# Four stages of an eight-stage transformer kernel re-arranged: ternary weights made beside the attention ahead, a local transformer's loads and residual beside its neighbours, its up-projection rests packed in one chunk, fourteen expert buffers

## The reference

```
x = x + L0_xattn(_layernorm(x), ctx)      # 16-head attention to 77 context rows
x = x + L0_ffn(_layernorm(x))             # ternary weights, 8-bit activations
x = x + L1_xattn(_layernorm(x), ctx)
x = x + L1_ffn(_layernorm(x))
x = x + L2_xattn(_layernorm(x), ctx)
x = x + L2_ffn(_layernorm(x))             # a whole local transformer, DEPTH = 6
x = x + L3_xattn(_layernorm(x), ctx)
x = x + L3_ffn(_layernorm(x))             # 64 experts, top 8, capacity 64
```

```
# L0_ffn: bitlinear(x, w) = act_quant(x) @ weight_quant(w).T
#   weight_quant: scale = 1 / clip(mean(|w|), 1e-5);  clip(round(w*scale), -1, 1) / scale
#   act_quant:    scale = 127 / clip(max(|x|, token), 1e-5); clip(round(x*scale), -128, 127) / scale
#   y = bitlinear(silu(bitlinear(x, w_gate)) * bitlinear(x, w_up), w_down)     inner width 1024
# L2_ffn: six times  x = x + local_attention(x);  then
#   hg = layernorm(x, g, bln) @ W1 + b1;  a, gate = split(hg)                  682 columns each
#   x = x + a * gelu(gate) @ W2 + b2
# L3_ffn: each token goes to 8 of 64 experts (256 -> 192 -> 256), their weighted results are summed
```

## Time and profile before

| | |
|---|---|
| median of three runs (lowest, highest) | 4475.44 us (4472.94, 4483.0) |
| the profiled execution: its time, its span | 4467.25 us, 4465.4 us |
| busy share of the span: PE, DVE, ACT, POOL | 89%, 56%, 44%, 33% |
| mean granted TensorE clock | 0.949 of full speed |
| share of the span of the DMA queue of SP | 13.2% |

### The profile page before, as it was taken

One profiled execution on the slowest core, in us unless ns is written; L12 is line 12 of the kernel. 1 busy time (PEld: TensorE's weight loads), 2 busy tenths in 40 slices (PEclk: granted clock), 3 DMA queues, 4 the chain that ended last, 5 costly groups with the idle time before them and its releaser, 6 DMA issues. The chain is left out here.

```text
span 4465.4 us, 70044 instructions
## 1 busy us (share of the span) xinstructions
PE 3960.8 (89%) x27065; PEld 2109.1 (47%) x27065; DVE 2515.2 (56%) x3505; ACT 1960.9 (44%) x3522; POOL 1468.7 (33%) x1326
## 2 busy tenths in 40 slices
PE   6767994869999999999999999999999999989564
PEld 4433431535554455445554455445554455435332
DVE  3583445548862588328862588328862588325522
ACT  3434544436643366326643366326643366314221
POOL 0000000016740376206640466206640467100044
PEclk9888997889999999999999999999999999999777
DMA  3000000021120111101120111101120111000377
GB/s 113 29 0 22 0 0 19 11 76 28 30 58 17 26 30 30 59 13 28 30 56 19 27 29 30 59 14 26 30 61 14 27 29 30 21 19 11 98 236 208
DMA packets 101435, 185.27 MB, mean 41 GB/s; under 512 B 13957, under 2 KB 54401, under 8 KB 100097
## 3 DMA queue, kind: packets, MB, share of 16 engines
q1 hardware_dynamic: 92912, 168.88, 13.2%
q0 software_dynamic: 6144, 9.44, 1.1%
q10 hardware_dynamic: 2064, 2.62, 0.2%
HBM read 112.06 MB, written 20.09 MB: 30 GB/s over the span
## 5 line engine op out<-in xcount | busy, mean ns | idle before, releaser
L1510 PE MATMUL PS<-locw,X 128*128 128x512 f32 x2304 | 1066.3, 599 | 43.9 <-PEq L1422 28.3
L1777 POOL TENSOR_TENSOR locm<-locm 128x512 f32<-128x512 f32 x384 | 488.1, 1271 | 920.2 <-DVE locm L1714 919.8
L1510 PEld LDWEIGHTS PS<-locw,X 128*128 128x128 f32 x2304 | 395.0, 190 | 456.6 <-issue 324.8
L1891 PE MATMUL PS<-locxn,locw 128*114 128x512 f32 (+1 forms) x1152 | 501.4, 593 | 13.4 <-DVE loch L2000 13.4
L1783 POOL TENSOR_TENSOR locm<-locm,locrn 128x512 f32<-128x512 f32 x384 | 392.4, 1043 | 129.0 <-ACT locrn L1629 129.0
L1790 POOL TENSOR_TENSOR locpr<-locpr,locrs 128x512 f32<-128x512 f32 x384 | 390.9, 1039 | 128.8 <-DVE locrs L1743 108.9
L1712 DVE TENSOR_TENSOR locm<-PS,loctab 128x512 f32<-128x512 f32 x384 | 263.6, 687 | 211.3 <-ACT locsq L1619 211.3
L1650 ACT ACTIVATE locpt<-PS 128x512 f32<-128x512 f32 x384 | 208.4, 594 | 321.8 <-PE PS L1520 321.8
L1891 PEld LDWEIGHTS PS<-locxn,locw 128*114 128x114 f32 (+1 forms) x1152 | 203.8, 178 | 306.8 <-issue 283.3
L2000 DVE SCALAR_TENSOR_TENSOR loch<-PS,locvec,locgl 114x512 f32<-114x512 f32 x144 | 107.0, 750 | 376.8 <-PE PS L1891 331.1
L1654 ACT ACTIVATE locpr<-locpr 128x1024 f32<-128x1024 f32 x192 | 203.3, 1059 | 191.4 <-DVE locpr L1734 191.4
(11 more groups left out here) (317 smaller groups left out, 6219.3 us busy)
## 6 DMA issues: line engine op xcount, KB each, us to landing
locve<-locva SPq DMA_DIRECT2D x372, 128.0 KB, 2.2
locw<-in_L2f_wqkv SPq DMA_DIRECT2D x36, 512.0 KB, 10.0
BIG<-in_L3f_gu SPq DMA_DIRECT2D x24, 768.0 KB, 5.6
BIG<-in_L3f_down SPq DMA_DIRECT2D x24, 384.0 KB, 6.9
moe_sums<-none SPq DMA_DIRECT2D x2, 4352.0 KB, 23.5
moeroom<-moe_sums SPq DMA_DIRECT2D x16, 512.0 KB, 6.9
locw<-in_L2f_w SPq DMA_DIRECT2D x6, 1364.0 KB
loctab<-in_L2f_tabs SPq DMA_DIRECT2D x6, 1024.0 KB, 10.3
```

The source lines that it names most:

```text
L1510: mm = pe.matmul(PS[:, o % 2, :], k.X[:, j, at - j:at - j + P], W[:, j, col:col + G], start=j == 0, stop=j == KD - 1)
L1777: pool.tensor_tensor(M1[:, j, :], M1[:, j, :], M2[:, x, :], ALU.add).then_inc(s.paired, 1)
L1891: mm = pe.matmul(PS[0:r, 4 + 2 * (m % 2) + half, :], W1[:, c, half * FI + m * FR:half * FI + m * FR + r], XNL[:, g % 2, c, :], start=c == ...
```

## The change

- **L0x and L0f.** The three weight loads are issued by SP behind L0x's own. DVE takes the three sums of absolute values in the steps of tiles 3, 4 and 5 of L0x, and the reciprocal in that of tile 7; POOL adds over the partitions and makes the ternary weights in BIG. L0f's first block is gone.
- **L0f's loop** is written out and deeper: gate and up in halves of 512 with their own semaphores, two buffers for most tiles, the x side done for two tiles at once, `down` three steps and `add` four steps behind. Scaling and rounding of x went from DVE to ACT (`raise_x`), of the hidden tile from DVE to POOL (`raise_h`), the small factors to POOL. PE turns XN directly.
- **L2f's start.** The layer norm is called by the stage, writes into X itself (`dest`), and SP's loads and POOL's mask cast and tables stand in its block; DVE waits there first for X to be saved.
- **L2f's up-projection.** Five chunks of 128 columns per half, and the two rests of 42 columns in one chunk: a in the rows 0 to 41, gate in the rows 64 to 105 of one bank, two matmuls for both.
- **L2f's end.** The saved residual is loaded in the last feed-forward block, once the attention outputs are used, and added there on DVE, four groups, ahead of `add_ffn(0)`; the last block is gone.
- **L3f.** WB = 14 and XB = 8. Nine pairs are loaded at once, four more after the rows are stored, one after the lists are made. The sums are read back into four buffers without a wait between the quarters, and with the four rows of a partition next to each other in memory.

```diff
@@ -125,7 +127,19 @@
+        def out_cols(b, h, c):
+            return k.XN[:, c, bass.ds(b * L + h * G, G)] if dest is None else dest[:, c, bass.ds(b * SEQ + h * G + 1, G)]
...
-                            op = dve.tensor_tensor(k.XN[:, c, bass.ds(b * L + h * G, G)], XC[:, h, c, :], RS[:, h, :], ALU.mult)
+                            op = dve.tensor_tensor(out_cols(b, h, c), XC[:, h, c, :], RS[:, h, :], ALU.mult)
...
@@ -550,6 +570,8 @@
                 for n in range(NT + 1):
                     if n + 1 < NT:
                         shift(n + 1)
+                    if beside:
+                        beside[2](dve, n)
                     for slot in "AB":
                         kind, g, c = slots.get((n, slot), (None, 0, 0))
                         if kind == "mean":
...
+def bitnet_weights(k, io):
+
+    s = Names()
+    s.loaded, s.sums, s.step, s.mean, s.scale = (k.sem("bit_weight_" + n) for n in ("loaded", "sums", "step", "mean", "scale"))
+    WF = [k.BIG[:, KD * T + i * 2048:KD * T + (i + 1) * 2048] for i in range(3)]
+    wq = k.BIG[:, KD * T + 3 * 2048:KD * T + 3 * 2048 + 3 * 1024].bitcast(BF16)
+    k.bit_wq = [wq[:, i * 2048:(i + 1) * 2048] for i in range(3)]
+
+    def load(sp):
+        for i, n in enumerate(("L0f_g", "L0f_u", "L0f_d")):
+            sp.dma_start(WF[i].rearrange("p (c n) -> p c n", c=io[n].shape[0] // P),
+                         io[n].rearrange("(c p) n -> p c n", p=P)).then_inc(s.loaded, 16)
+
+    def quantise(pool):
+        count = [0]
+
+        def link(op):
+            count[0] += 1
+            op.then_inc(s.step, 1)
+            pool.wait_ge(s.step, count[0])
+
+        pool.wait_ge(s.sums, 3)
+        link(pool.partition_all_reduce(k.bit_sum[:, 3:6], k.bit_sum[:, 0:3], P, RSUM))
+        link(pool.tensor_scalar(k.bit_mean[:, :], k.bit_sum[:, 3:6], 1.0 / (D * FF), 1e-5, ALU.mult, ALU.max))
+        pool.sem_inc(s.mean, 1)
+        pool.wait_ge(s.scale, 1)
+        for i in range(3):
+            link(pool.tensor_scalar(WF[i], WF[i], k.bit_scale[:, i:i + 1], ROUND, ALU.mult, ALU.add))
+            link(pool.tensor_scalar(WF[i], WF[i], ROUND, 1.0, ALU.subtract, ALU.min))
+            link(pool.tensor_scalar(k.bit_wq[i], WF[i], -1.0, None, ALU.max))
+
+    def measure(dve, n):
+        if 3 <= n < 6:
+            i = n - 3
+            dve.wait_ge(s.loaded, 48)
+            dve.tensor_reduce(k.bit_sum[:, i:i + 1], WF[i], AX.X, ALU.add, apply_absolute_value=True).then_inc(s.sums, 1)
+        if n == 7:
+            dve.wait_ge(s.mean, 1)
+            dve.reciprocal(k.bit_scale[:, :], k.bit_mean[:, :]).then_inc(s.scale, 1)
+
+    return load, quantise, measure
+
+
 def stage_bitnet_ffn(nc, k, io):
...
+                def raise_h(n):
+                    pool.wait_ge(s.h_scaled, n + 1)
+                    if n >= 2:
+                        pool.wait_ge(s.hq, n - 1)
+                    pool.tensor_scalar(HR[:, n % 2, :], H[:, n % 2, :, :].rearrange("p j n -> p (j n)"), HS[:, 2, n:n + 1], ROUND,
+                                       ALU.mult, ALU.add).then_inc(s.hr, 1)
+                    pool.tensor_scalar(HS[:, 3, n:n + 1], HS[:, 1, n:n + 1], k.bit_mean[:, 2:3], None, ALU.mult).then_inc(s.h_factor, 1)
...
+                def measure_h(n):
+                    dve.wait_ge(s.h, 2 * n + 2)
+                    dve.tensor_reduce(HS[:, 0, n:n + 1], H[:, n % 2, :, :].rearrange("p j n -> p (j n)"), AX.X, ALU.max,
+                                      apply_absolute_value=True).then_inc(s.h_step, 1)
+                    dve.wait_ge(s.h_step, 2 * n + 1)
+                    dve.tensor_scalar(HS[:, 1, n:n + 1], HS[:, 0, n:n + 1], 1e-5, 1.0 / 127.0, ALU.max, ALU.mult).then_inc(s.h_step, 1)
+                    dve.wait_ge(s.h_step, 2 * n + 2)
+                    dve.reciprocal(HS[:, 2, n:n + 1], HS[:, 1, n:n + 1]).then_inc(s.h_scaled, 1)
+
+                def clip_h(n):
+                    dve.wait_ge(s.hr, n + 1)
+                    if n >= 2:
+                        dve.wait_ge(s.hqt, n - 1)
+                    dve.tensor_scalar(HQ[:, n % 2, :], HR[:, n % 2, :], ROUND, 127.0, ALU.subtract, ALU.min).then_inc(s.hq, 1)
...
+                for n in range(NT + 4):
+                    if n >= 4:
+                        add(n - 4)
+                    if n < NT:
+                        hidden(n, 0)
+                        hidden(n, 1)
+                    if 1 <= n <= NT:
+                        clip_h(n - 1)
+                    if n and n % 2 == 0 and n // 2 + 1 < MX:
+                        clip_x(n // 2 + 1)
+                    if n < NT:
+                        measure_h(n)
+                    if n % 2 and n // 2 + 2 < MX:
+                        measure_x(n // 2 + 2)
...
@@ -1335,7 +1393,10 @@
 TILES = L // P
 FI = D * 4 * 2 // 3
 FM = -(-FI // P)
-FR = -(-FI // FM)
+FR = P
+FL = FI - (FM - 1) * P
+GATE_AT = 64
+F1 = 2 * (FM - 1) * P + GATE_AT + FL
 MASKED = -1e30
...
-        with nc.Block() as block:
-            @block.sync
-            def _(sp):
-                sp.dma_start(kept, Xf).then_inc(kept_saved, 16)
-                sp.dma_start(MASKF, io["L2f_mask"]).then_inc(s.mask_loaded, 16)
-                load_layer(sp, 0)
-
-            @block.gpsimd
-            def _(pool):
-                make_tables(pool, 0)
-
-            @block.vector
-            def _(dve):
-
-                for q in (s.centred, s.log_var):
-                    dve.sem_inc(q, 1)
-                for q in (s.h, s.x1, s.x2):
-                    dve.sem_inc(q, 2)
-                dve.wait_ge(s.mask_loaded, 16)
-                dve.tensor_copy(MASKB[:, :, :], MASKF)
-                dve.wait_ge(kept_saved, 16)
-                for b in range(B):
-                    dve.tensor_copy(k.X[:, :, b * SEQ + 1:b * SEQ + 1 + L], k.XN[:, :, b * L:(b + 1) * L])
+        beside = Names()
+
+        def load_first(sp):
+            sp.dma_start(kept, Xf).then_inc(kept_saved, 16)
+            sp.dma_start(MASKF, io["L2f_mask"]).then_inc(s.mask_loaded, 16)
+            load_layer(sp, 0)
+
+        def make_first(pool):
+            pool.wait_ge(s.mask_loaded, 16)
+            pool.tensor_copy(MASKB[:, :, :], MASKF)
+            make_tables(pool, 0)
+
+        def begin(dve):
+            for q in (s.centred, s.log_var):
+                dve.sem_inc(q, 1)
+            for q in (s.h, s.x1, s.x2):
+                dve.sem_inc(q, 2)
+            dve.wait_ge(kept_saved, 16)
+
+        beside.load, beside.make, beside.begin = load_first, make_first, begin
+        stage_layernorm(nc, k, k.X, dest=k.X, beside=beside)
 
         for layer in range(DEPTH):
             with ExitStack() as actx:
...
                             load_layer(sp, layer + 1)
+                        else:
+                            sp.wait_ge(s.x1, KD * (n0 + NG) + KD)
+                            sp.dma_start(XB, kept).then_inc(kept_back, 16)
 
                     @block.gpsimd
...
-                            for m in range(FM):
-                                r = rows(m)
+                            for m in range(FM - 1):
                                 pe.wait_ge(s.h, FM * (n0 + g) + m + 1)
                                 for half, ready in ((1, s.gate_in_psum), (0, s.a_in_psum)):
+                                    at = half * (FM - 1) * P + m * P
                                     for c in range(KD):
-                                        mm = pe.matmul(PS[0:r, 4 + 2 * (m % 2) + half, :], W1[:, c, half * FI + m * FR:half * FI + m * FR + r],
+                                        mm = pe.matmul(PS[:, 4 + 2 * (m % 2) + half, :], W1[:, c, at:at + P],
                                                        XNL[:, g % 2, c, :], start=c == 0, stop=c == KD - 1)
                                     mm.then_inc(ready, 1)
+                            pe.wait_ge(s.h, FM * (n0 + g) + FM)
+                            for c in range(KD):
+                                mm = pe.matmul(PS[0:GATE_AT + FL, LAST, :], W1[:, c, 2 * (FM - 1) * P:F1],
+                                               XNL[:, g % 2, c, :], start=c == 0, stop=c == KD - 1)
+                            mm.then_inc(s.gate_in_psum, 1)
 
                         def down(g):
                             pe.wait_ge(s.h, FM * (n0 + g) + FM + 2)
@@ -1951,9 +2019,12 @@
                         def gelu(g):
...
+                        def add_kept(g):
+                            x, y = k.X[:, :, tokens(g)], XB.rearrange("p (c t) -> p c t", c=KD)[:, :, tokens(g)]
+                            dve.wait_ge(kept_back, 16)
+                            dve.tensor_tensor(x, x, y, ALU.add).then_inc(kept_added, 1)
...
+                        if layer == DEPTH - 1:
+                            for g in range(NG):
+                                add_kept(g)
...
-        with nc.Block() as block:
-            @block.sync
-            def _(sp):
-                sp.dma_start(XB, kept).then_inc(kept_back, 16)
-
-            @block.vector
-            def _(dve):
```

(20 more changed lines are left out.)

428 lines of the change are left out of this document (217 added, 211 removed).

## The result

The changed kernel takes 4349.64 us, the median of four runs (4335.02 to 4358.58), where the kernel before, measured beside it, takes 4474.82 (four runs, 4472.94 to 4483.0): a ratio of 0.9724, 95% interval 0.9707 to 0.9742, or 125 us less where 161.8 were summed.

| stretch | before | after | moved | summed |
|---|---|---|---|---|
| start to L0f's layer norm | 184.1 | 184.6 | +0.5 | +3.5 |
| L0f | 175.9 | 126.3 | -49.6 | -53.0 |
| L1x | 300.7 | 300.6 | -0.1 | 0 |
| L1f and L2x | 278.4 | 289.2 | +10.8 | 0 |
| L2f's start | 49.9 | 29.9 | -20.0 | -19.5 |

What follows compares the result with a forecast made beforehand. Six places, each with its own limit (such as PE in L2f, DVE in L0f's loop, DMA in L3f); the terms summed to -161.8 us from the profiled 4467.3: 4305.5, median 4314. Range 4282 to 4352, about 8 in 10.

Steps and rivals of the forecast that it cites:

- the first rival: L3f stays bound by its indirect transfers, gathers and scatters setting the pace; this place gives 5 us: 4349; chance 0.15.
- L0f's weights: L0f's first stretch of 30.9 us, with PE idle and a load waited for, nearly all goes: -30.5 us.
- L0x's cost: In L0x DVE gets three reductions of 2.29 us, partly hidden: +3.5 us, bounds 0 and 6.9.
- L0f's loop: Work taken off DVE brings L0f's pace from 6.80 to 5.3 us a tile: -22.5 us, bounds 27 and 0.
- L2f's start: Transfers move 23 us ahead to the layer norm's first moment, so the first projection starts earlier: -19.5 us.
- L2f's feed-forward: Each up in L2f loses four passes, 1.72 us, less a longer wait in up(1): -35 us, bounds 30 and 41.
- L2f's end: The wait of 7.95 us and the addition of 4.43 go, the new additions hidden beside down(0): -12.3 us.
- L3f's pairs: With 18 pairs reloaded instead of 25, DMA work ends the last scatter near 4372: -40 us, bounds 10 and 52.
- L3f's tail: Reading back the sums takes 25 us from about 4420, last quarter near 4446 instead of 4451.7: -5.5 us.
- Handoffs in L0f: Rival: waits on POOL and on PE's turn behind clip_x eat the L0f gain, pace 6.8 us: 4336; chance 0.09.
- POOL blocking DVE: Rival: POOL passes and two-SBUF-input DVE products exclude each other in L0x and L2f's first layer norm, +9: 4323; chance 0.10.
- The clock in L2f: Rival "slower": PE's granted clock falls in L2f under denser work; at 0.90, +333 us: 4647; chance 0.02.

Runs made afterwards that it cites:

- save_wait_later: Changed kernel with the wait for the residual's save moved from the first centring to the first write into X in L2f's first layer norm: 4340.51 us.
- tables_first: save_wait_later with the tables and their rows loaded ahead of the projection weights: 4344.87 us, one run.
- combined: Changed kernel with 128-row last down chunk, two reloads outstanding at most, later save wait, tables' product in first attention block, packed chunk third: 4306.28 us.
- packed_first: Changed kernel with the packed chunk of 42 linear and 42 gate rests computed first in each up() instead of last: 4379.64 us, one run.

## Why the prediction was right or wrong

The time lies inside the stated range, but only 2.4 us below its upper end, and 36 above the sum. It equals the 4349 of the first rival by luck: that rival took everything outside L3f's pairs as summed, and the layers missed by 20 us. One of the prediction's own signs of being wrong came true: gathers landed 9.3 us after their issue, where it had drawn the line at 8.

**L0f's weights (-30.5)**: right. From the layer norm's first centring to the first hidden product it was 58.1 us and is 27.2: -30.9.

**L0x's cost (+3.5)**: too high, it is 1.4. The end of L0x doesn't show it: the next layer norm begins at 184.1 and 187.7 in two profiles of before and between 178.2 and 188.2 in those of the changed program. But from the third on, the distances between DVE's reductions of the scores (L519, now L539) repeat to 0.02 us in all fourteen profiles, in before and after alike, except for the four in which the new reductions (88.7, 94.3, 101.2) lie or are made up for: these are 24.75 us together in both profiles of before and 26.15 to 26.16 in all twelve of the changed program. Of 3 x 2.28 us the slack took 5.4. POOL's passes ended in time, although two of their rates, taken from a copy and a product, were wrong.

**L0f's loop (-22.5)**: right, 5.36 us a tile instead of 5.3, -21.6. What I left as it was, the tail, grew: from the last hidden product to the next centring 15.8 us became 18.7, +2.9; there is one hop more over POOL and the product comes in halves, but no run tells what did it.

**L2f's start (-19.5)**: right, -20.0, by the steps given.

**L2f's feed-forward (-35)**: the step that failed is "It loses four passes: 1.72 us, 24 times", in what it left out: the same packing gives `down` a chunk of 42 rows among chunks of 128, which I didn't price. `up` gained 1.61 and `down` lost 0.67 a group, the wait in `up(1)` the forecast 1.1 a layer. That is 4 x (1.61 - 0.67) - 1.1 = 2.6 a layer, 16 in all; the layers without a dip of the clock say 501.6 - 498.7 = 2.9. With 128 rows in each chunk a layer takes 495.8: the 5.8 a layer that I had. The Trainium skill ("TensorE: Matmul & The Clock Gate", LDWEIGHTS (loading the stationary operand)) says that a load's time goes by columns, not by rows; the trace agrees, 184 ns for 42 rows and 190 for 128, but the cost lies between a load of 128 rows and one of 42, not in either load. Between 114 and 112 rows there was none; where the cost begins no run tells.

**L2f's end (-12.3)**: right. From the last feed-forward addition to L3x it was 16.3 us and is 4.0. The other 2.4 us of that row are the clock at L3x's opening.

**L3f's pairs (-40)**: wrong in size, -21. The step is "18 x 3.45 + 32 x 1.35 = 105 us of DMA, at 95% busy 111": it spread the transfers over all pairs. The reloads stand in the first part instead: from 4184 to 4270 us the engines are full, and the scatters of 16 pairs pass, at 5.3 us; only then the other pairs run at POOL's 3.3, with the engines half idle. That is my first rival in kind: scatters landed 10.0 us after issue, and each waited for the one two pairs before. I gave it 5 us and a chance of 0.15. The term itself was low, too: 18 pairs' weights took 73.0% of 95 us, 69 us or 3.85 a pair instead of 3.45. The caps show that both the backlog and the plain DMA work bind: two reloads at a time give 2 to 10 us back, one at a time moves the wait to the weights. That the row buffers brought the larger part I had in one sentence ("let a gather take its 6.7 us under other pairs") and without a price. By the Trainium skill's rule ("DMA: Bandwidth & Descriptors", Queues, rings and completion order) that an engine takes turns between queues by packets, a deeper backlog would not lengthen a gather; the landings say otherwise: 7.8 us with two reloads outstanding and 9.3 without a bound, the engines full in both, and 4.8 with one, the engines not quite full.

**L3f's tail (-5.5)**: right, 49.6 to 43.7 from last scatter to end: -6.0.

**The other rivals.** Handoffs in L0f: didn't come, but for the tail. POOL blocking DVE: beside POOL's product of two tiles it is real, as save_wait_later, tables_first and `combined` show, and L2f's layer norm missed it by 0.07 us. Beside POOL's one-input passes it is not: in L0x the DVE product at 128.48 us lay inside such a pass and kept its 1.23 us, and so did its like in the eleven other profiles of the changed program. The Trainium skill's rule ("SBUF — State Buffer", Who interferes with whom) that the prediction tells agrees with the 4.99 us; for the passes of L0x, which read SBUF too, the measurement says otherwise. The clock in L2f stayed at its upper level but for the dips named above.

Of 161.8 us, 20 went to the feed-forward's layers, 18 to L3f, 3 to L0f, and the row up to L0f's layer norm gave 3 back, 2 of them the smaller cost in L0x. Without the openings of L2x and L3x at the low level the profiles would differ by 123; the medians differ by 125.

## What to carry to other kernels

When a split is changed to make one matmul cheaper, look at every matmul that the same split shapes: zero rows up to a full chunk cost nothing here, and neither did 114 beside 112 rows, but 42 beside 128 did. A sum of DMA work is a bound only over the stretch in which that work is asked for; where transfers with a dependency between them share the engines with bulk loads, bound the bulk in flight, and give buffers to the short transfers first. Compare stretches, and know how far the same stretch moves by itself, before a difference of a few microseconds is called a gain. Before a step is pulled forward, see what will run beside it there: DVE's products of two SBUF tiles must not meet a POOL product of two tiles. And when POOL's first tensor operation behind an all-reduce is moved, some 7 to 11 us ahead of it move along.

## What the runs showed of the hardware that I had not expected

POOL's tensor-scalar with 2048 columns takes 1.9 to 2.0 us with two operations (multiply and add, minimum and maximum), 5.4 with one, and 7.1 with subtraction first of two. A matmul group whose chunks have 128, 42 and again 128 rows loses 0.3 to 0.4 us at each such chunk; one of 114 and 112 rows loses nothing. A DVE product of two SBUF tiles took 4.99 us instead of 0.69 beside a POOL product, and its usual 1.23 inside a POOL pass with one input. The same instructions, reached at the same time, open L2x at 1.2 or at 2.4 GHz from one execution to the next, worth 10 us, and L3x, which with what leads to it took 148.7 to 160.2 us in those twelve profiles, likewise. So does L0x: with a granted clock of 0.97 from 40 to 60 us its first reduction of the scores starts at 57.2 us (save_wait_later), with 0.70 at 66.7 (packed_first). These openings and the dips in L2f's layers, each worth up to 10 or 12 us, make up much of the scatter of these times. And between `partition_all_reduce` and a tensor operation on POOL stands an instruction, MODIFY_POOL_CONFIG, behind which the next one began 6.7 to 10.8 us later; why this time differs between the places stays open.
